# Two normalising passes put on the scalar engine and the feed-forward outputs rotated over four PSUM banks, in an eight-core attention and feed-forward layer

## The reference

```python
def _L0_ffn_ref(hidden_states, gate_w, up_w, down_w, fc1_w, fc2_w, expert_w, ...):
    routing_weights, _ = top_k(einsum('bsh,he->bse', hidden_states, gate_w), 2)
    h = relu(einsum('bsh,hi->bsi', hidden_states, up_w)) ** 2
    shared_out = einsum('bsi,ih->bsh', h, down_w)
    x_latent = einsum('bsh,hl->bsl', hidden_states, fc1_w)
    expert_out = einsum('bsl,lm->bsm', x_latent, expert_w)
    moe_out = expert_out * sum(routing_weights, axis=-1, keepdims=True)
    routed_out = einsum('bsl,lh->bsh', moe_out, fc2_w)
    return _layernorm(shared_out + routed_out, ln_gamma, ln_beta)

x = x + _layernorm(_L0_attn_ref(_layernorm(x), ...))
x = x + _layernorm(_L0_ffn_ref(_layernorm(x), ...))
```

## Time and profile before

| | us |
|---|---|
| median of 2 runs | 5265.57 |
| the two runs | 5149.15 and 5381.99 |
| the profiled execution | 4919.78 |
| its span, first to last instruction, slowest core | 4918.7 |
| spans of the 8 cores | 4887.6 to 4918.7 |

### The profile page before, as it was taken

One profiled execution on the slowest core, in us unless ns is written; L12 is line 12 of the kernel. 1 busy time (PEld: TensorE's weight loads), 2 busy tenths in 40 slices (PEclk: granted clock), 3 DMA queues, 4 the chain that ended last, 5 costly groups with the idle time before them and its releaser, 6 DMA issues.

```text
span 4918.7 us, 43172 instructions; the slowest of 8 cores (4887.6 to 4918.7 us)
## 1 busy us (share of the span) xinstructions
PE 3870.2 (79%) x18033; PEld 1729.4 (35%) x18033; DVE 761.7 (15%) x1126; ACT 488.8 (10%) x797; POOL 269.1 (5%) x369
## 2 busy tenths in 40 slices
PE   1699999999549712889998999971589998999960
PEld 1244444444223201334443444430234443444430
DVE  4300000000460143110000000007310000000027
ACT  2100000002213411001111000002001111000001
POOL 0000000000000022000000000000000000000000
PEclk9999999999759855799999999995799999999985
DMA  5144444446002234569998878863569887777743
GB/s 157 38 75 75 76 75 75 75 76 103 0 1 44 77 146 162 111 117 154 152 153 137 139 135 139 141 129 97 118 117 154 153 152 138 141 133 143 140 89 120
DMA packets 69743, 548.40 MB, mean 111 GB/s; under 512 B 7146, under 2 KB 7594, under 8 KB 21931
## 3 DMA queue, kind: packets, MB, share of 16 engines
q0 software_dynamic: 57552, 444.68, 52.7%
q1 hardware_dynamic: 12000, 100.96, 5.7%
HBM read 948.33 MB, written 41.94 MB: 201 GB/s over the span
## 4 chain that ended last, share of the span: by engine, by line
PE 74%; DVE 11%; DMA 9%; issue 2%; POOL 1%; SPq 1%; ACT 1%; DVEq 0%; ACTq 0%; POOLq 0%
PE ps L964 21%; PE ps L442 20%; PE ps L1119 18%; DVE pool L179 11%; PE ps L1057 5%; PE ps L705 2%; DMA pool<-fc1w 2%; DMA pool<-x 2%; PE ps L1019 1%; POOL pool L775 1%; PE ps L708 1%; PE ps L511 1%; DMA pool<-expw 1%; DMA pool<-x2sp 1%; DMA pool<-fc2w 1%
## 5 line engine op out<-in xcount | busy, mean ns | idle before, releaser
L964 PE MATMUL ps<-pool 128*128 128x512 bf16 x5120 | 1128.5, 383 | 192.8 <-DVE pool L179 139.0
L442 PE MATMUL ps<-pool 128*128 128x512 bf16 x4608 | 998.1, 379 | 0.9 <-DVE pool L179 0.9
L1119 PE MATMUL ps<-pool 128*128 128x512 bf16 x4096 | 898.4, 380 | 44.0 <-DMA pool<-fc2w 43.7
L964 PEld LDWEIGHTS ps<-pool 128*128 128x128 bf16 x5120 | 503.7, 99 | 819.6 <-issue 232.9
L442 PEld LDWEIGHTS ps<-pool 128*128 128x128 bf16 x4608 | 445.4, 97 | 553.4 <-issue 3.6
L179 DVE CAST pool<-ps 128x512 bf16<-128x512 f32 (+1 forms) x192 | 107.2, 558 | 3332.0 <-PE ps L1057 1992.3
L1119 PEld LDWEIGHTS ps<-pool 128*128 128x128 bf16 x4096 | 396.8, 98 | 523.4 <-issue 51.0
L179 ACT ACTIVATE pool<-pool 128x512 bf16<-128x512 f32 (+4 forms) x251 | 232.0, 924 | 1978.0 <-DVE pool L179 1809.1
L179 ACT ACTIVATE pool<-ps 128x512 f32<-128x512 f32 (+1 forms) x256 | 152.9, 597 | 1331.5 <-PE ps L964 1221.6
L1057 PE MATMUL ps<-pool 128*128 128x512 bf16 x1024 | 231.5, 379 | 0.0
L179 DVE TENSOR_TENSOR pool<-pool 128x1 f32<-128x1 f32 (+3 forms) x226 | 173.4, 767 | 252.1 <-ACT pool L179 187.8
(11 more groups left out here) (63 smaller groups left out, 954.1 us busy)
## 6 DMA issues: line engine op xcount, KB each, us to landing
pool<-upw POOLq DMA_DIRECT2D x128, 1024.0 KB, 10.1
pool<-downw POOLq DMA_DIRECT2D x64, 2048.0 KB, 15.2
pool<-wconv POOLq DMA_DIRECT2D x72, 1024.0 KB, 16.8
pool<-x SPq DMA_DIRECT2D x16, 2048.0 KB, 9.6
pool<-fc1w POOLq DMA_DIRECT2D x32, 1024.0 KB, 9.4
pool<-fc2w POOLq DMA_DIRECT2D x32, 1024.0 KB, 19.6
x2sp<-pool SPq DMA_DIRECT2D x8, 2048.0 KB, 6.3
pool<-expw POOLq DMA_DIRECT2D x16, 1024.0 KB, 9.5
```

The costliest lines, as they stand in the source:

```text
L442: it = te.matmul(pbf[bk], sl[:, k * 128 : (k + 1) * 128], t1T[:, k * 1026 + base : k * 1026 + base + 512], start=(dw == 0 and k == 0), sto ...
L964: it = te.matmul(pbf[bk], slots[s][:, k * 128 : (k + 1) * 128], rhs_fn(k), start=(k == 0), stop=(k == n_k - 1))
L1119: te.matmul(pbf[bk], dw_sl[s][:, k * 128 : (k + 1) * 128], hup[:, k * 512 : (k + 1) * 512], start=(k == 0), stop=False)
```

## The change

It has two parts. In the norm stage both normalising passes leave DVE and become ACT instructions of the form scale*x + bias, with the scale 1/sqrt(var) and the bias -mean/sqrt(var). The bias takes two more 128x1 ACT instructions each time. The statistics of step 2 get columns of their own for odd and even tiles, and the waits are set to match: ACT now waits for the store that DVE waited for. In the feed-forward, the chunks of fc1, expert, up and down go over four banks in turn and not over two; `gate_top2`, which uses banks 2 and 3 too, waits for them.

```diff
     def f_part1(t):
         par = t % 2
+        mu_p, var_p, r_p, nmr_p = 50 + par, 52 + par, 54 + par, 56 + par
...
         p.wait(ve, "SV", a_ready)
-        ve.tensor_scalar(stat(S_MU), stat(S_ASUM + t), 1.0 / D, None, ALU.mult)
...
+        p.wait(ve, "SC", cg_par[par])
+        ve.tensor_scalar(stat(mu_p), stat(S_ASUM + t), 1.0 / D, None, ALU.mult)
...
-        c_r = p.inc(se.activation(stat(S_R), stat(S_R), AF.Exp, bias=0.0, scale=-0.5), "SC")
-        p.wait(ve, "SC", c_r)
-        p.wait(ve, f"SS{par}", x2_spilled[par])
-        iv = ve.tensor_scalar(x2t[par], a_tm[t], stat(S_MU), stat(S_R),
-                              ALU.subtract, ALU.mult)
-        c_g = p.inc(iv, "SV")
-        p.wait(po, "SV", c_g)
+        se.activation(stat(r_p), stat(r_p), AF.Exp, bias=0.0, scale=-0.5)
+        se.activation(stat(nmr_p), stat(mu_p), AF.Identity, bias=0.0, scale=stat(r_p))
+        se.activation(stat(nmr_p), stat(nmr_p), AF.Identity, bias=0.0, scale=-1.0)
+        p.wait(se, f"SS{par}", x2_spilled[par])
+        p.wait(se, "SV", ve_x2done[par])
+        ia = se.activation(x2t[par], a_tm[t], AF.Identity,
+                           bias=stat(nmr_p), scale=stat(r_p))
+        c_g = p.inc(ia, "SC")
+        cg_par[par] = c_g
+        p.wait(po, "SC", c_g)
...
         c_r2 = ln_stats_fast(x2t[par], t2s[par], trashF)
-        p.wait(ve, "SC", c_r2)
-        iv = ve.tensor_scalar(t2s[par], x2t[par], stat(S_MU), stat(S_R),
-                              ALU.subtract, ALU.mult)
-        c_t2s[t] = p.inc(iv, "SV")
+        ve_x2done[par] = p.cnt["SV"]
+        se.activation(stat(S_NMR), stat(S_MU), AF.Identity, bias=0.0, scale=stat(S_R))
+        se.activation(stat(S_NMR), stat(S_NMR), AF.Identity, bias=0.0, scale=-1.0)
+        ia = se.activation(t2s[par], x2t[par], AF.Identity,
+                           bias=stat(S_NMR), scale=stat(S_R))
+        c_t2s[t] = p.inc(ia, "SC")
...
             p.wait(te, "SV", c_rw)
+            if tl == 0:
+                p.wait(te, *bank_free[2])
+                p.wait(te, *bank_free[3])
...
-                bk = m % 2
+                bk = m % 4
```

More of the change, by code:

```diff
@@ L300, in build @@
     S_SUM, S_SQ, S_MU, S_VAR, S_R, S_NEGM, S_L, S_M1, S_M2, S_RW = range(10)
+    S_NMR = 10
     def finish():
@@ L753, in build @@
     c_spills = {}
+    ve_x2done = [0, 0]
+    cg_par = [0, 0]
     def f_part1(t):
         par = t % 2
+        mu_p, var_p, r_p, nmr_p = 50 + par, 52 + par, 54 + par, 56 + par
         p.wait(sy, "SG", xin_free[par])
@@ L759, in f_part1 @@
         p.wait(ve, "SV", a_ready)
-        ve.tensor_scalar(stat(S_MU), stat(S_ASUM + t), 1.0 / D, None, ALU.mult)
-        ve.tensor_tensor(stat(S_VAR), stat(S_MU), stat(S_MU), ALU.mult)
-        iv = ve.tensor_scalar(stat(S_VAR), stat(S_ASQ + t), 1.0 / D, stat(S_VAR),
+        p.wait(ve, "SC", cg_par[par])
+        ve.tensor_scalar(stat(mu_p), stat(S_ASUM + t), 1.0 / D, None, ALU.mult)
+        ve.tensor_tensor(stat(var_p), stat(mu_p), stat(mu_p), ALU.mult)
+        iv = ve.tensor_scalar(stat(var_p), stat(S_ASQ + t), 1.0 / D, stat(var_p),
                               ALU.mult, ALU.subtract)
@@ L765, in f_part1 @@
         p.wait(se, "SV", c_v)
-        se.activation(stat(S_R), stat(S_VAR), AF.Ln, bias=EPS, scale=1.0)
-        c_r = p.inc(se.activation(stat(S_R), stat(S_R), AF.Exp, bias=0.0, scale=-0.5), "SC")
-        p.wait(ve, "SC", c_r)
-        p.wait(ve, f"SS{par}", x2_spilled[par])
-        iv = ve.tensor_scalar(x2t[par], a_tm[t], stat(S_MU), stat(S_R),
-                              ALU.subtract, ALU.mult)
-        c_g = p.inc(iv, "SV")
-        p.wait(po, "SV", c_g)
+        se.activation(stat(r_p), stat(var_p), AF.Ln, bias=EPS, scale=1.0)
+        se.activation(stat(r_p), stat(r_p), AF.Exp, bias=0.0, scale=-0.5)
[8 more added lines that the diff above has]
+        p.wait(po, "SC", c_g)
         p.wait(po, f"SX{par}", c_load)
@@ L783, in f_part1 @@
         c_r2 = ln_stats_fast(x2t[par], t2s[par], trashF)
-        p.wait(ve, "SC", c_r2)
-        iv = ve.tensor_scalar(t2s[par], x2t[par], stat(S_MU), stat(S_R),
-                              ALU.subtract, ALU.mult)
-        c_t2s[t] = p.inc(iv, "SV")
+        ve_x2done[par] = p.cnt["SV"]
[4 more added lines that the diff above has]
+        c_t2s[t] = p.inc(ia, "SC")
     def f_part2(t):
         par = t % 2
-        p.wait(te, "SV", c_t2s[t])
+        p.wait(te, "SC", c_t2s[t])
         p.wait(te, f"SS{par}", c_spills[t])
```

## The result

The changed kernel is a little faster: the ratio of its time to that of the kernel before is 0.9949, with a 95% interval of 0.9937 to 0.9961. That is 25 us of the median of 4931.77 us that thirteen runs of the kernel before gave; the changed kernel's median over fourteen runs is 4902.56. The profiled executions took 4919.78 us before and 4905.72 after, with spans of 4918.7 and 4904.7 us.

A forecast was written before the change was run, and what follows sets the result against it. TensorE is busy for 79% of the span, so only its waits can be won: 20.7 us (norm stage) + 14.3 (banks) = 35.0 less, 4884.8 for the profiled execution, 0.71%, carried over to 5228 us; range 4870 to 5345.

The forecast's parts named there:

- The absolute time: Whole kernel: 4884.8 us for an execution like the profiled one, 5228 us as the forecast time.
- I carry the share over to their median: Whole kernel: the 0.71% gain applied to the median of two timed runs, 5265.57 x 0.9929 = 5228 us.
- The second pass leaves DVE: Norm stage: copies come 3.2 us earlier in tiles 2 to 7, 19.4 us, plus 2.9 in the last tile.
- The first pass leaves DVE: Norm stage: ACT's longer pass hidden under the load of x, costing nothing except 1.6 us in the first tiles.
- Four banks: fc1, half 1: four chunks instead of two before the stall, one pair dropped afterwards; gain 14.3 us, nothing elsewhere.
- I take 2 us, with 0 and 6.8 as bounds: Final norm beside fc1's stall: cost of one x2 load on DVE's path meeting chunk 4's load.
- The upper figure of 19 for the gain: fc1's stall in half 1: the banks' gain of 14.3 us was put between 9.6 and 19.
- rival 1: Norm stage: x loads at 13.49 us take back 4.3 us a tile; total -9 us, 5256; chance 0.08.
- a load of x over 12 us in the later tiles: Norm stage: one of the signs listed as showing the forecast wrong.
- Rival 2: fc1, half 1: stores or weights, not the bank, hold chunk 2; only 20.7 us gained, 4899.1 or 5243; chance 0.08.
- Rival 3: Norm stage, ACT: the passes' length decides, 3.9 us a tile; total +17.2 us, 4937.0 or 5284; chance 0.07.
- Rival 4: Down stage: four banks remove all 72.2 us of PE's wait before the transposes; 4812.6 or 5151; chance 0.02.

## Why the prediction was right in direction and wrong in size

**The absolute time.** 5228 us came from carrying the share to the median of two runs; it missed, while 4884.8 for an execution like the profiled one is 18 us from the median of 4902.56. The step that failed is "I carry the share over to their median": thirteen runs of the kernel before put its median at 4931.77 us, not 5265.57. The profiled time was the better base, and the range held the result only because it was made wide enough for both. The forecast also took 2% for "about what a measurement of this kernel can tell from no change". The change stayed within the 2%, but its ratio is known to 0.12% either way, so a quarter of that can be told.

**The second pass leaves DVE: right.** 22.3 us forecast, 21.5 to 22.4 measured outside the loads' times, by the same steps: 3.2 us in each tile, ACT's pass of 3.80 us hidden.

**The first pass leaves DVE: right, and a term too small.** Nothing in tiles 2 to 7. In the second tile the 1.6 us were worked out against the slowest core's load, which had been late (POOL's start 13.6 us after the issue); against a load in time the ten instructions cost 3.1 us (15.57 less 12.50), and 2.3 in the mean of the cores. The other loads took 1.6 us more in their sum, which the forecast had put at nothing. Together, 21.5 less 2.3 less 1.6: 17.5 measured for 20.7.

**Four banks: the mechanism right, one term mis-sized.** The pair of chunks was worth 16.35 us in the forecast; over the eight runs with four banks and the five with two, the go-on to the expert stage took 102.3 and 117.7 us in the mean, 15.4 less. The step that failed is "I take 2 us, with 0 and 6.8 as bounds" for the load of x2 that meets the load of chunk 4. It costs 8 to 13 us, 10 in the mean, in the cores where chunk 4's load is issued first, and that is most of them. In the mean of the five executions with four banks that leave these loads as they are, the stall is 7.5 us longer (164.5 against 157.0 in the five with two), more than the upper bound of 6.8. That bound doubled the transfer, as if two took turns; no row of the trace before has a load issued behind a weight load that had just started. The upper figure of 19 for the gain has no working in the forecast, where 16.35 with the bound of 0 is the most. With 15.4 - 7.5 = 7.9 us for 14.3, and 17.5 for 20.7, the sum is 25.4 us, and the timed difference is 25, with 19 to 31 as its interval. That they meet so closely is partly luck, since single executions of the same code differ by up to 6 us in fc1 of half 0 alone.

**The rivals.** The loads of x took back 1.6 us in all and not 4.3 a tile, so rival 1 fell as a size. There is something in it: a load of x over 12 us in the later tiles was named as a sign of being wrong, and from issue to POOL's start tile 2's took 12.06 and 13.12 us in two of the eight cores, and over 12 in four with the norm stage's part alone, where the most before is 11.35. In that run the loads of tiles 2 to 7 took 5.5 us more than before in their sum. Rival 2 fell by the fourth chunk in the stall. Rival 3, the pass's length on the path, is false for this kernel and true for the next one: once the loads are out of the way, ACT's pass costs 11.6 us more than DVE's in this stage. This is where the rule of the Trainium skill ("ScalarE: Activation LUTs", Rules for kernel authors), that additions and multiplications belong on VectorE, comes out right: for the first pass, not for the second. For the second, what stands behind it on DVE's list outweighs the 1.4 us of DVE's speed. Rival 4 named the right gap, and its reason against held: banks don't close it and the order does.

## What to carry to other kernels

Ask of a unit of work not which engine does it faster, but what stands behind it on that engine's list and whether the path runs through it; here the same move was worth 22 us for one pass and nothing for its twin. Where work is let into a stall, look at whose end the stall waits for and what the work's own transfers will meet there, above all which is issued first; half the gain of the two added banks went that way. And when PE waits for the copy of what it has just made, write the next block of matmuls in between before adding banks: here 83 us for a reordering, and none for the banks.

## What the runs showed of the hardware

- A 1 MB load of f32 by SP took 13.2 to 19.7 us from issue to use (17.4 in the mean of 25 cores) when a weight load by POOL had been issued 2.8 to 4.7 us ahead of it, and 7.2 to 14.5 (10.0 in the mean of 15) when it was issued 0.6 to 2.7 us ahead of the weight load. The order of issue made 7 us of difference in the mean; whether the descriptors' queue or the transfer itself does it, these runs don't tell.
- An ACT pass over 128x4096 with scale and bias from columns takes 3.80 us in every core of the changed kernel; a square of the same size, without the columns, takes 3.62.
- The load of 2 MB of x takes from 9.2 to 13.2 us from issue to POOL's start in tiles 2 to 7, by core and execution. The sum of the eight times was 77 to 99 us over the cores of all executions that leave these loads as they are, and up to 16 us apart between the cores of one. What of it is made by the other cores' traffic was not tried.
